# Third attention layer: context projections moved into the rounding stage, kept in DRAM; value projections taken one batch ahead

## What is computed

```python
ln_out = ln(x) * ln_w + ln_b
q, k, v, qx = [round_fp8(ln_out / in_scale) @ w.T * scale for each]
kx, vx = split(cond @ w_kv_x.T)          # the context projections
q, k, qx, kx = ln over each head of 128
core = attention(q, k, v)                # 8 groups, 2 heads each
xout = attention(qx, kx, vx)
out = round_fp8(concat(core, xout) / smooth) @ wproj.T * scales
```

## Time and profile before

| | us |
|---|---|
| median of 3 runs (range) | 1830.45 (1828.95 to 1835.7) |
| the profiled execution: its own time / span on the core | 1835.48 / 1833.7 |
| rounding stage, ACT's first to DVE's last instruction | 864.6 to 898.5 |
| main loop, PE's first matmul to the last addition to `x` | 899.7 to 1307.3 |

### The profile page before, as it was taken

How to read it: one execution, slowest core, us unless ns; L and a number is a source line. 1 busy time by engine, 2 the same in 40 slices (tenths; PEclk the granted TensorE clock), 3 DMA queues, 4 the chain that set the end, 5 groups by cost and what they waited for, 6 DMA issues and landing times. The chain is left out here.

```text
span 1833.7 us, 25059 instructions
## 1 busy us (share of the span) xinstructions
PE 1525.9 (83%) x8562; PEld 980.8 (53%) x8600; DVE 1080.1 (59%) x2317; ACT 804.5 (44%) x1879; POOL 794.2 (43%) x959
## 2 busy tenths in 40 slices
PE   7566659999797799997399999999799989836772
PEld 5222235656464365655167777777455555525661
DVE  7999961223674643355778888888722255462336
ACT  3989862110333211112488888888521112412221
POOL 3367641000200299791277777777210000027772
PEclk9655659999697999998699999999899988858796
DMA  2499871110504011320200000000111100156656
GB/s 78 89 177 182 172 162 33 36 42 18 184 2 167 27 48 65 115 66 25 68 2 1 1 1 1 1 1 1 44 30 43 35 25 1 46 195 233 231 171 238
DMA packets 174223, 140.12 MB, mean 76 GB/s; under 512 B 141793, under 2 KB 154721, under 8 KB 170386
## 3 DMA queue, kind: packets, MB, share of 16 engines
q1 hardware_dynamic: 165314, 114.89, 22.0%
q0 software_dynamic: 6416, 22.03, 3.6%
q10 hardware_dynamic: 2368, 1.61, 0.3%
HBM read 85.43 MB, written 19.50 MB: 57 GB/s over the span
## 5 line engine op out<-in xcount | busy, mean ns | idle before, releaser
L389 PE MATMUL l1e_gu<-x_normT,l1e_w 128*128 128x512 f32 x384 | 171.6, 602 | 0.0
L1859 POOL CAST l0m_pi<-l0m_pf 128x1024 bf16<-128x1024 int16 x128 | 133.2, 1040 | 87.0 <-ACT l0m_pf L1926 85.4
L1451 PE MATMUL l2x_pr<-l_w,l2x_xq 128*128 128x512 bf16 x538 | 133.6, 385 | 37.8 <-ACT credits L42 35.9
L1926 ACT ACTIVATE l0m_pf<-l0m_s,l0m_bias,l0x_sq 128x1024 int16<-128x1024 f32 x128 | 153.9, 1204 | 19.2 <-DVE l0m_bias L1957 12.6
L1953 DVE TENSOR_REDUCE l0m_mx<-l0m_s 128x1 f32<-128x1024 f32 x128 | 155.6, 1215 | 4.7 <-PE l0m_s L1868 4.4
L1868 PE MATMUL l0m_s<-l0x_kT,l0x_qT 64*128 64x512 bf16 x256 | 70.6, 575 | 64.7 <-ACT l0m_pf L1926 63.5
L389 PE MATMUL l0e_gu<-x_normT,l0e_w 128*128 128x512 f32 x272 | 121.3, 601 | 0.0
L1578 DVE BATCH_NORM_STATS2 l2x_bn<-l2x_raw 128x6 f32<-128x128 f32 x384 | 83.3, 279 | 64.3 <-ACT l2x_raw L1519 64.3
L389 PEld LDWEIGHTS l1e_gu<-x_normT,l1e_w 128*128 128x128 f32 x384 | 74.2, 194 | 84.2 <-issue 83.1
L389 PE MATMUL l2e_gu<-x_normT,l2e_w 128*128 128x512 f32 x256 | 114.3, 602 | 0.0
L441 ACT ACTIVATE l1e_sil<-l1e_gu 128x512 f32<-128x512 f32 x48 | 28.6, 596 | 178.6 <-PE l1e_gu L389 178.6
(11 more groups left out here) (505 smaller groups left out, 3608.1 us busy)
## 6 DMA issues: line engine op xcount, KB each, us to landing
l3m_w<-in_l_moe SPq DMA_DIRECT2D x16, 1280.0 KB, 6.9
l1e_w<-in_l_ffn SPq DMA_DIRECT2D x24, 384.0 KB, 3.1
l_rows<-zero_row SPq DMA_DIRECT2D x8, 1024.0 KB, 10.9
l_w<-l_rows SPq DMA_DIRECT2D x8, 1024.0 KB, 12.7
l0e_w<-in_l_ffn SPq DMA_DIRECT2D x17, 384.0 KB, 3.1
l2e_w<-in_l_ffn SPq DMA_DIRECT2D x16, 384.0 KB, 3.1
ctx_tok<-l_route SPq DMA_DIRECT2D x8, 512.0 KB
l2q_wps<-in_l_wp SPq DMA_DIRECT2D x16, 256.0 KB, 2.8
```

Of the source, the lines that this page charges most:

```text
L389: last = nc.tensor.matmul(gu[half][:, m, :], w[:, c % SW, (2 * k + m) * P:(2 * k + m + 1) * P], pg.xnT[:, k, cols(n)], start=(k == 0), sto ...
L1451: last = nc.tensor.matmul(flat(pr[t % 2][:]), src[:, k, tokens], pg.l2_w3[:, part, k, at:at + W], start=(k == 0 and part == 0), stop=(k == ...
L1859: nc.gpsimd.tensor_copy(pi[:, n % 8, :], pf[:, n % 4, :]).then_inc(s["rounded"], 1)
L1926: nc.scalar.activation(pf[:, n % 4, :], s_ps[n % 3][:], ACT.Exp, scale=sq[:, h, b:b + 1], bias=bias[:, n % 4:n % 4 + 1], accum_out=sm[:, b ...
```

## The change

In the rounding stage PE now runs all 32 context projections (4 per batch) into eight PSUM banks; ACT copies each into one of four slots `kv`, and POOL stores the slot to a DRAM tensor `l2_kv`. ACT's order is: after each of its sixteen weight pieces in the job loop one copy (14 of them), then the last two pieces, then the other 18 copies. In the main loop SP loads them back, per batch two pieces `kx` and two `vx`, double-buffered in the space of `l2_wx`. Statistics and normalising of `kx` read the loaded tile. Steps 6 and 7 lose their projections in every phase but the first; steps 0 and 1 of a side-1 phase project the values `v` of the next batch, so every phase but the first and the last has six projections of 6 bf16 matmuls.

```diff
+            @block.tensor
+            def _(pe):
+                for i in range(KV_STEPS):
+                    b, u = divmod(i, 4)
+                    if i >= 8:
+                        pe.wait_ge(kv_kept, i - 7)
+                    for k in range(KD):
+                        last = nc.tensor.matmul(kv_ps[i % 8][:], pg.ctxT[:, k, b * P:(b + 1) * P], pg.l2_wx[:, k, u * W:(u + 1) * W],
+                                                start=(k == 0), stop=(k == KD - 1))
+                    last.then_inc(kv_done, 1)
+            @block.gpsimd
+            def _(pool):
+                for i in range(KV_STEPS):
+                    pool.wait_ge(kv_kept, i + 1)
+                    pool.dma_start(pg.l2_kv[i], kv[:, i % 4]).then_inc(kv_stored[i % 4], 16)
...
+                def keep_kv(i):
+                    act.wait_ge(kv_done, i + 1)
+                    if i >= 4:
+                        act.wait_ge(kv_stored[i % 4], 16 * (i // 4))
+                    nc.scalar.activation(kv[:, i % 4], kv_ps[i % 8][:], ACT.Copy).then_inc(kv_kept, 1)
...
                             keep(q)
+                            keep_kv(q)
                 keep(14)
                 keep(15)
+                for i in range(14, KV_STEPS):
+                    keep_kv(i)
...
+            def source(it, t):
+                if t >= 6 or (it[1] == 1 and t < 2):
+                    return V_, it[0] + it[1], t % 2
+                return (QX if it[1] else K_ if t < 2 else Q_), it[0], None
+            def projects(it, t):
+                if it is None:
+                    return False
+                if t >= 6:
+                    return it == (0, 0)
+                return it != (B - 1, 1) or t >= 2
+            def values(it):
+                return vx[:, it[0] % 2] if it[1] else pg.xnT[:, it[0] % 2]
+            @block.sync
+            def _(sp):
+                for b in range(B):
+                    for i in range(4):
+                        sp.wait_ge(kv_stored[i], 16 * (b + 1))
+                    if b >= 2:
+                        sp.wait_ge(s["normed"], item((b - 2, 1)) * 6 + 2)
+                    for u in range(2):
+                        sp.dma_start(kx[:, b % 2, u], pg.l2_kv[4 * b + u].rearrange("p (j d) -> p j d", j=U)).then_inc(kx_in[b % 2], 16)
+                    if b >= 2:
+                        sp.wait_ge(s["valued"], item((b - 2, 1)) * 4 + 4)
+                    for u in range(2):
+                        sp.dma_start(vx[:, b % 2, u * W:(u + 1) * W], pg.l2_kv[4 * b + 2 + u]).then_inc(vx_in[b % 2], 16)
...
-                            else:
-                                at = t * W if t < 2 else (t - 4) * W
-                                for k in range(KD):
-                                    last = nc.tensor.matmul(flat(pr[t % 2][:]), pg.ctxT[:, k, tokens], pg.l2_wx[:, k, at:at + W],
-                                                            start=(k == 0), stop=(k == KD - 1))
+                        if projects(pi, t):
+                            pe.wait_ge(s["raw"], projected(pi, t) + 1)
+                            which, batch, part_v = source(pi, t)
...
+                            if source(pi, t)[0] != V_:
+                                dve.wait_ge(s["raw"], projected(pi, t) + 3)
+                                rows = raw[:, t]
+                            else:
+                                dve.wait_ge(kx_in[pi[0] % 2], 16 * 2 * (pi[0] // 2 + 1))
+                                rows = kx[:, pi[0] % 2, t]
```

More of the change, by code:

```diff
@@ L1283, in attention_l2 @@
         wp_in = [pg.sem(f"l2q_wp_in{i}") for i in range(4)]
+        kv_done, kv_kept = pg.sem("l2q_kv_done"), pg.sem("l2q_kv_kept")
+        kv_stored = [pg.sem(f"l2q_kv_stored{i}") for i in range(4)]
+        KV_STEPS = 4 * B
         with ExitStack() as st:
@@ L1292, in attention_l2 @@
             wps = sb("wps", [P, 4, 2, D])
+            kv = sb("kv", [P, 4, W])
+            kv_ps = [st.enter_context(nc.psum_tensor(f"l2q_kv_ps{i}", [P, W], F32)) for i in range(8)]
             block = st.enter_context(nc.Block())
@@ L1341, in attention_l2 @@
                  "recip", "p_normed", "p_turned", "p_kept", "valued", "o_read", "qsteps2", "widened", "quanted", "y_done", "y_added", "aff_in", "aggr", "y_scale", "smooth")
+        kx_in, vx_in = ([pg.sem(f"l2x_{m}_in{i}") for i in range(2)] for m in ("kx", "vx"))
         s = {m: pg.sem(f"l2x_{m}") for m in names}
@@ L1441, in fn @@
                     for t in range(8):
[L1442 to L1448, removed]
-                                for k in range(KD):
-                                    for part in range(3):
-                                        last = nc.tensor.matmul(flat(pr[t % 2][:]), src[:, k, tokens], pg.l2_w3[:, part, k, at:at + W],
-                                                                start=(k == 0 and part == 0), stop=(k == KD - 1 and part == 2))
-                            else:
-                                at = t * W if t < 2 else (t - 4) * W
-                                for k in range(KD):
-                                    last = nc.tensor.matmul(flat(pr[t % 2][:]), pg.ctxT[:, k, tokens], pg.l2_wx[:, k, at:at + W],
-                                                            start=(k == 0), stop=(k == KD - 1))
+                        if projects(pi, t):
+                            pe.wait_ge(s["raw"], projected(pi, t) + 1)
+                            which, batch, part_v = source(pi, t)
+                            tokens = slice(batch * P, (batch + 1) * P)
+                            src = xq[:, which]
+                            at = 3072 + part_v * W if which == V_ else 4096 + (t - 2) * W if which == QX else t * W
+                            for k in range(KD):
+                                for part in range(3):
+                                    last = nc.tensor.matmul(flat(pr[t % 2][:]), src[:, k, tokens], pg.l2_w3[:, part, k, at:at + W],
+                                                            start=(k == 0 and part == 0), stop=(k == KD - 1 and part == 2))
                             last.then_inc(s["proj"], 1)
@@ L1512, in fn @@
                     for t in range(8):
[L1513 to L1519, removed]
+                        if projects(pi, t):
+                            act.wait_ge(s["proj"], projected(pi, t) + 1)
+                            which, batch, part_v = source(pi, t)
+                            dst = pg.xnT[:, batch % 2, part_v * W:(part_v + 1) * W] if which == V_ else flat(raw[:, t])
+                            nc.scalar.activation(dst, flat(pr[t % 2][:]), ACT.Copy, scale=scales[:, which:which + 1]).then_inc(s["raw"], 1)
                         if job := due(t, 3, ai, zi, wi):
```

24 lines of the change are left out of this document (17 added, 7 removed).

## The result

The changed kernel takes **1846.35 us** (median; 1844.27 to 1856.67), the kernel before 1829.22 beside it: ratio **1.0102**, 95% interval 1.0079 to 1.0125. It is 17.1 us slower, where the forecast said 7.6 and held "within 0.5%" for a little likelier than "slower". The sign was right; the size, 1.0%, is twice the 0.5% that the prediction took for the least that a measurement can tell. The time lies inside the range of 1820 to 1850.

A forecast was written before the change was run, and what follows sets the result against it. PE bounds the loop before; after the change a chain through ACT, DVE and POOL does. Rounding stage +22.9, loop −14.3, clock at the loop's start −1.0 sum to +7.6 us: 1838.1 from 1830.45, range 1820 to 1850.

The forecast's parts named there:

- within 0.5%: Whole kernel: a time within 0.5%, 9.2 us, of the kernel before; chance 0.46.
- slower: Whole kernel: slower than the kernel before by more than 0.5%; chance 0.43.
- The chain: Loop: a fixed 15.26 us through ACT, DVE and POOL closes each phase, so 1.00 us a phase is saved, 14.3 together.
- The turn of the stage takes 1.18 us: Rounding stage's end: 1.18 us after POOL's last issue at 921.4 the loop starts, 22.9 us later than before.
- The clock in the loop: Main loop after its start: no cost of a lower clock was counted.
- The clock at the loop's start: Loop's first matmuls, before at 1.2 GHz: a gain between 0 and 2.6 us, taken as 1.0.
- The sum: Whole kernel: +22.9 rounding stage, −14.3 loop, −1.0 clock at the loop's start, together +7.6 us.
- The stores: Rounding stage: POOL's stores take 4 us from copy to landing, at no cost; 6.2 would slow PE.
- the held stores: Rival, rounding stage: POOL's stores get through once per DVE job, 11.6 us more, 1850; chance 0.12.

The follow-up runs named there:

- e1_warm: The changed kernel with four idle bf16 matmuls on PE in each of the emptied steps 6 and 7; 9.8 us over the kernel before (1.0055).
- e7_turn_later: The changed kernel with PE's turn of each normalised piece and ACT's copy of it one step later; 13.5 us over the kernel before.
- e2_half: Half the move: 16 of 32 context projections in the rounding stage, no look-ahead of `v`; 3.7 us under the kernel before (0.9974).
- e6_stores_sp: The changed kernel with the rounding stage's 32 stores issued by SP instead of POOL; 6.6 us over the kernel before.
- e3_rounding_alone: The kernel before with only the changed rounding stage, its old loop reading nothing of what is stored; 27.6 us over the kernel before.
- e9_both_terms: The changed kernel with SP issuing the stores and four idle matmuls in each of steps 6 and 7; 5.6 us over the kernel before (1.0022).
- e11_no_normalising: e7_turn_later without POOL's normalising of the probabilities, so part of the computation is left out; 19.0 us under the kernel before.

## Why the prediction was too low

- **The chain was right.** "The change gives 1.00 us a phase instead of 3.44": with the clock held 0.97 (e1_warm) or 0.88 (e7_turn_later); the chain measured 15.25 us against 15.26; PE's idle was 2.11 us where 2.4 was said, and with the 0.15 it stands in the two places named. The additions drew together by 11.3 us in e1_warm, where 12 were forecast, and the whole loop there saved 16.6 us (407.04 − 390.41) where 14.3 + 1.0 were counted. That half the move wins less than the chain allows (e2_half) is open.
- **"The turn of the stage takes 1.18 us" failed.** I read that from a stage in which POOL did nothing, and carried it to one that POOL ends with a DMA. I even put POOL's last issue on the path, and stopped at its end. From there to PE's first matmul it was 4.03 us (923.52 to 927.55), 3.36 of them POOL's leaving; the stage became 25.5 us longer, not 22.9. e6_stores_sp shows it: with the stores on SP the stage is 21.9 us longer.
- **The clock in the loop failed: it was put at nothing without a reason.** I said "clock" of the rounding stage and of the loop's start only, and took 2.4 GHz in the loop for granted because before had it throughout. But before had PE busy 48.43 of 48.69 us; the change makes PE idle in every phase, and I had forecast that idle time myself. Holding the clock gave back 6.2 us between the additions and 6.6 in the whole loop (e1_warm).
- **The clock at the loop's start was about right.** The loop ran its first 3.65 us at 1.2 GHz, before 5.3; with the old loop behind the new stage that won 0.85 us (e3_rounding_alone), where 1.0 was taken. Without POOL's longer turn 1.7 more would have come (first addition after 84.50 us in e9_both_terms, 86.23 in e1_warm), together the 2.6 that was the most it could be.
- **The sum.** Forecast +7.6; the turn +2.7 and the clock in the loop +6.6, less the 1.3 us by which the loop with the clock held was better than counted, make +15.6, which the trace has. The last 1.5 to 4 us are in the rest of the program.
- **The stores** were rightly costed at nothing: issue 0.54 to 0.67 us beside DVE's work, landing 2.3 on the median, 5.6 at most. The rule of the Trainium skill that I had made a rival of ("SBUF — State Buffer", section "Summary: rules for kernel authors": GpSimd's descriptor writing starves beside VectorE's fast modes) did not show in this trace: from 894.50 to 897.03 three stores landed in 2.3 us each with DVE busy (4.73 us of the 4.90 from 894.5 to 899.4). The 3.5 to 5.6 us of the first twelve go with the loads beside them. POOL's queue was the wrong one all the same, for another reason: the turn. A small misreading: ACT copies a context projection in 0.60 us, not in the 0.69 of the earlier trace rows, which are scaled copies.
- **Chances.** "Slower" had 0.43. The two missed terms both worked one way. That 1846 lies inside the range is luck: its upper end came from a rival, the held stores, that had nothing to do with them.

## What to carry over

When a change makes the bounding engine idle, the forecast owes a term for what that idleness itself costs: here TensorE lost its clock in time that looked free, and idle matmuls won 6.6 us back in the traces (e1_warm against the changed kernel), 7 to 9 by the medians. Cost the end of a stage by the engine that now leaves it last, not by the turn that was there. And where a chain closes the loop, moving half of the work took three quarters of the gain of a batch and, hidden under another engine's work, cost the stage nothing.

## What the runs showed of the hardware

- **Leaving a stage after POOL's DMAs** took 3.36 us of POOL in the changed kernel. In e2_half POOL's last issue ended at 900.16 and DVE worked until 902.95, which covered the leaving: the stage took no longer than before. After SP's stores ACT began the loop 0.77 us after its last copy.
- **Short idle times cost the clock.** With 2.1 us of idle before a turn in each phase of 23.5 us, the grant fell to 1.2 GHz for 3.4 us in four of the five heavy batches, which took 1.0 to 1.3 us longer; each fall began within 0.4 us of the end of such an idle time. With four idle matmuls in each empty step it never did. In e7_turn_later PE was idle nearly as long, 3.8 us a heavy batch against 4.4, but in pieces of at most 0.98 us, and the grant held in all five.
- **A short DVE step is held up beside POOL.** L1257 takes 0.29 us; in a batch of e7_turn_later it took 1.01 the four times that POOL's normalising ran beside it. Without that normalising (e11_no_normalising) all eight took 0.29.
- **The rest of the program varies with the clock too.** The same code takes 519 to 532 us from the last addition to the end. In the shortest (e11_no_normalising, 519.4) PE is busy 397.1 us at a mean grant of 0.86, in the changed kernel (530.3) 408.8 us at 0.83, both with 1824 matmuls. Two windows, each 19.5 us from 0.5 us behind the last addition's start, the kernel before:

```profile
1307.30:1326.80 19.50, 14.93 (x58) 10.61 (x59) 10.30 (x63) 8.78 (x17) 0.14 (x1) 0.64 0.31 102
```

and the changed kernel:

```profile
1325.10:1344.60 19.50, 14.90 (x53) 11.63 (x54) 8.11 (x39) 8.36 (x16) 0.14 (x1) 0.51 0.30 102
```

The clock was 0.64 in the one and 0.51 in the other, and DVE got 63 instructions done against 39. Why the grant differs there between kernels was not found.
